# A gated delta-rule layer on one core: the second head's batches exchanged, products on all four quarters of the array, the decayed state made on GpSimd

## The reference, cut to what matters

```python
# x: 8 batches of 512 tokens, D = 256; 16 key heads, 32 value heads (2 per key head), head size 128, chunks of 64 tokens
qkvz = x @ W_qkvz                                   # per key head: q, k, two v, two z
q, k, v = silu(causal_conv1d(...)); g = cumulated log decay; beta = sigmoid(...)
attn = inverse of the unit lower triangle from k_beta k^T * decay_mask          # 64 by 64 for each chunk
for c in range(8):                                  # chunks, one after the other
    v_prime = value_corrected[c] - k_cumdecay[c] @ state
    out = (q[c] @ state) * g_exp + (q[c] k[c]^T * decay_mask) @ v_prime
    state = state * g_exp_last + (k[c] * k_decay)^T @ v_prime
out = rmsnorm(out * silu(z)) @ W_out
```

## Time and profile before

| | us |
|---|---|
| median of 3 runs | 4962.62 (4961.7 to 4965.15) |
| the profiled execution, its time | 4955.99 |
| its span, first to last instruction | 4954.2 |
| PE busy | 4628.7 (93%) |
| DVE busy | 3573.7 (72%) |
| ACT busy | 3072.0 (62%) |
| POOL busy | 694.4 (14%) |
| mean granted TensorE clock | 0.986 |

### The profile page before, as it was taken

The page is one execution under the profiler, slowest core; times in us unless marked ns, Lnnn a source line. Parts: engine busy times, 40 slices in busy tenths (PEclk is TensorE's granted clock), DMA queues, the critical chain, the costliest instruction groups (busy, mean ns, idle before and its releaser), DMA issues.

```text
span 4954.2 us, 144941 instructions
## 1 busy us (share of the span) xinstructions
PE 4628.7 (93%) x54288; PEld 3167.2 (64%) x54320; DVE 3573.7 (72%) x7576; ACT 3072.0 (62%) x7979; POOL 694.4 (14%) x680
## 2 busy tenths in 40 slices
PE   4998999999999899999999899999999899999998
PEld 2555666666666566666666566666666666666666
DVE  7554677777777677777777677777777677777776
ACT  2333666666666566666666566666666566666665
POOL 0000111111111111111111111111111111111111
PEclk8999999999999999999999999999999999999999
DMA  2111222222223222222223222222223222222221
GB/s 61 41 35 63 63 69 55 60 66 61 68 56 77 66 69 53 61 66 61 69 50 79 69 61 56 65 66 62 56 60 82 68 59 58 64 67 61 69 59 34
DMA packets 760100, 305.22 MB, mean 62 GB/s; under 512 B 672880, under 2 KB 716016, under 8 KB 749168
## 3 DMA queue, kind: packets, MB, share of 16 engines
q1 hardware_dynamic: 620144, 287.40, 23.5%
q10 hardware_dynamic: 139264, 8.42, 1.8%
HBM read 216.96 MB, written 66.07 MB: 57 GB/s over the span
## 4 chain that ended last, share of the span: by engine, by line
issue 56%; PE 27%; POOL 8%; DVE 4%; ACT 2%; DMA 1%; SPq 1%; POOLq 0%; DVEq 0%; ACTq 0%
PE pj L660 5%; POOL rout L1559 4%; PE dsb L819 3%; PE pj L655 2%; POOL gb L1550 2%; POOL kn L1555 2%; PE pot L605 2%; PE dsb L791 1%; PE pot L777 1%; PE ms L693 1%; PE pod L803 1%; PE ms L589 1%; PE pot L748 1%; PE pj L589 1%; PE pod L760 1%
## 5 line engine op out<-in xcount | busy, mean ns | idle before, releaser
L660 PE MATMUL pj<-xnT,wt 128*128 128x512 f32 x2048 | 1022.2, 622 | 34.0 <-DMA cw<-in_L_attn_conv_weight 20.6
L1292 DVE SCALAR_TENSOR_TENSOR cy<-xpad,cw,cy 128x1024 f32<-128x1024 f32 x768 | 976.2, 1278 | 7.9 <-ACT cy L1003 0.9
L1559 POOL TENSOR_TENSOR rout<-rin,expo 128x2 f32<-128x2 f32 x512 | 358.3, 700 | 3737.4 <-DVE rin L1443 3737.4
L1429 DVE SCALAR_TENSOR_TENSOR st<-st,gel,dsb 128x128 f32<-128x128 f32 x1536 | 430.9, 343 | 288.0 <-PE dsb L791 285.1
L819 PE MATMUL dsb<-wo,yT 128*128 128x256 f32 x2048 | 575.0, 403 | 13.2 <-issue 12.1
L660 PEld LDWEIGHTS pj<-xnT,wt 128*128 128x128 f32 x2048 | 351.7, 191 | 363.8 <-issue 349.0
L1002 ACT ACTIVATE xpad<-pj 128x512 f32<-128x512 f32 x512 | 305.5, 597 | 359.1 <-PE pj L660 359.1
L655 PE MATMUL pj<-wt,xnT 128*128 128x256 f32 x2048 | 509.9, 392 | 0.0
L1062 ACT ACTIVATE yT<-dsb 128x256 f32<-128x256 f32 x512 | 203.2, 397 | 469.0 <-PE dsb L810 467.5
L819 PEld LDWEIGHTS dsb<-wo,yT 128*128 128x128 f32 x2048 | 348.0, 189 | 117.8 <-issue 89.6
L655 PEld LDWEIGHTS pj<-wt,xnT 128*128 128x128 f32 x2048 | 368.3, 189 | 84.6 <-issue 44.3
(11 more groups left out here) (174 smaller groups left out, 8009.7 us busy)
## 6 DMA issues: line engine op xcount, KB each, us to landing
qge<-ge_rows SPq DMA_DIRECT2D x64, 1024.0 KB, 7.1
wt<-in_L_attn_W_qkvz SPq DMA_DIRECT2D x64, 768.0 KB
gb<-g_rows SPq DMA_DIRECT2D x128, 256.0 KB
a_d<-at SPq DMA_DIRECT2D x64, 512.0 KB, 2.6
wo<-in_L_attn_W_out SPq DMA_DIRECT2D x64, 256.0 KB, 2.7
x_d<-xpair SPq DMA_DIRECT2D x128, 128.0 KB, 1.8
ap_<-a_d SPq DMA_DIRECT2D x512, 16.0 KB, 1.8
dd<-x_d SPq DMA_DIRECT2D x512, 16.0 KB, 2.1
```

Source lines behind the costliest of these rows:

```text
L660: last = mm(pj[n % 2][:, :], wt[:, k, col:col + DH], batch(xnT, k, i), start=(k == 0), stop=(k == KD - 1))
L1292: stt(y, x[:, :, tap:tap + SEQ], cw[:, kind, tap:tap + 1], y, ALU.mult, ALU.add).then_inc(S["conv"], 1)
L1429: last = stt(st[:, (c + 1) % 2, b, h, :], st[:, c % 2, b, h, :], gel[:, p, h, b * NC + c:b * NC + c + 1], dsb[:, b, h * DH:(h + 1) * DH], ...
L1559: tt(rout[:, :], rin[:, :], expo[:, 0, 0:GRP], ALU.pow).then_inc(S["routs"], 1)
```

## The change: what it does, and the diff

1. For the second value head (h = 1) the two batches change places in the residual, in W and in the gated output (`home`). `solve` and `intra` then use all four 64 by 64 tiles: h = 0 on the diagonal, h = 1 off it, into another PSUM bank. The banks are laid out anew (`quad`). `key_state` becomes four products of 128 columns for two of 256, with the batches of h = 1 picked in exchanged order.
2. `output_rows` turns h = 1 back: it is now a product with an identity whose halves are exchanged (`cst[:, h*CH:...]`), and for h = 0 with the plain identity, in place of two transposes.
3. z is projected as before; ACT writes it exchanged. A z eviction of 128 by 512 becomes one of 128 by 2x128 and two of 64 partitions. For the first z fill (chunks 0, 1) the second part stands behind the SiLU and the squares of k, and `pcopy` counts only after it. The v evictions become four of 128 by 128 for two of 128 by 256. The v1 convolution holds its batches in exchanged places.
4. `update_state` was four instructions (state times decay plus increment, 128 by 128 each). POOL now multiplies the state by its decay (`decay_state`, chunks 1 to 6), and DVE adds the increment in one instruction.
5. The first fixpoint round no longer waits for the DMAs of eturn (DVE's second `add_round` does) but for all three negated copies. `decayed_squares(1)` moves from piece 18 to 17, one convolution tap from 17 to 18, and the first two `add_round` from piece 20 to 21, behind the residual of chunk 7.
6. In `last_tile` and at chunk 0 some waits move; the setup's layouts of g and of the columns change with the new order of units.

```diff
-        dsb = ctx.enter_context(nc.psum_tensor("dsb", [P, NB, 512], F32))
-        pch, pds = dsb[:, 0, :], dsb[:, 1, :]
-        pot = bank("pot")
-        pod = bank("pod")
-        pkw, po = pot, pod
+        quad = ctx.enter_context(nc.psum_tensor("quad", [P, 4, 512], F32))
+        pot, pod, pch, pds = (quad[:, n, :] for n in range(4))
+        po = quad[:, 0:2, DH:2 * DH]
+        pod_rows = quad[:, 0, 2 * DH:2 * DH + D]
+        pw = quad[:, 1:3, 0:DH]
+        pks = quad[:, 2, 0:GRP * DH]
+        pyt = quad[:, 3, 0:GRP * DH]
+        pstate = quad[:, 2:4, GRP * DH:2 * GRP * DH]
...
-                    loaded(pe, d_et, g, GRP * NBLK)
-                    after(pe, "pneg", g, 2)
+                    after(pe, "pneg", g, 3)
                 else:
                     after(pe, "yadd", g, 2 * r)
-                    if r == 1:
-                        after(pe, "pneg", g, 3)
                 apart(pe)
                 src = yy if r else ee
                 for v in range(8):
                     cut = slice(v * CH, (v + 1) * CH)
                     for b in range(NB):
                         straight = tile_product(ms[0][half(b), cut], b, pbd[half(b), v, :], src[half(b), v, :], b)
-                        if r == 1:
-                            turned = tile_product(ms[1][half(1 - b), cut], 1 - b, pback[half(b), v, :],
-                                                  yy[half(b), 8 + v, :], b)
-                        else:
-                            rhs = yy[half(1 - b), 8 + v, :] if r else eturn[half(1 - b), v, :]
-                            turned = tile_product(ms[1][half(b), cut], b, pbd[half(1 - b), 8 + v, :], rhs, 1 - b)
+                        lhsT = pback[half(b), v, :] if r == 1 else pbd[half(b), 8 + v, :]
+                        turned = tile_product(ms[1][half(1 - b), cut], 1 - b, lhsT, src[half(b), 8 + v, :], b)
...
             def key_state(g, p, c):
                 after(pe, "ss_", g, c)
                 apart(pe)
-                for b in range(NB):
-                    last = mm(pkw[half(b), 0:GRP * DH], kq[:, p, c, b, :],
-                              st[:, c % 2, b, :, :].rearrange("p h d -> p (h d)"), start=True, stop=True,
-                              tile_position=(0, b * CH))
+                for h in range(GRP):
+                    for b in range(NB):
+                        last = mm(pks[half(b), h * DH:(h + 1) * DH], kq[:, p, c, home(b, h), :],
+                                  st[:, c % 2, home(b, h), h, :], start=True, stop=True, tile_position=(0, b * CH))
                 last.then_inc(S["ks"], 1)
...
-                for h in range(GRP):
-                    for b in range(NB):
-                        rhs = rr[half(b), h, :] if c else vb[p][half(b), h, :]
-                        last = mm(pkw[half(b), (GRP + h) * DH:(GRP + h + 1) * DH], bda[half(b), p, c * GRP + h, :],
-                                  rhs, start=True, stop=True, tile_position=(b * CH, b * CH))
+                for a in range(NB):
+                    for h in range(GRP):
+                        rhs = rr[half(a), h, :] if c else vb[p][half(a), h * NC, :]
+                        last = mm(pw[half(home(a, h)), h, :], bda[half(a), p, h * NC + c, :], rhs,
+                                  start=(c == 0 or h == 1), stop=True, skip_group_check=True,
+                                  tile_position=(a * CH, home(a, h) * CH))
...
             def intra(g, p, c):
-                if c == 0:
-                    before(pe, "og", g)
                 if c == NC - 1:
                     after(pe, "wev", g, NC)
+                    after(pe, "accs", g, c - 3 + 1)
                 apart(pe)
-                for h in range(GRP):
-                    for b in range(NB):
-                        last = mm(po[half(b), h * DH:(h + 1) * DH], it[half(b), p, c * GRP + h, :], ww[half(b), h, :],
-                                  start=(c == 0), stop=True, skip_group_check=True, tile_position=(b * CH, b * CH))
+                for b in range(NB):
+                    for h in range(GRP):
+                        last = mm(po[half(home(b, h)), h, :], it[half(b), p, h * NC + c, :], ww[half(b), h, :],
+                                  start=(c == 0), stop=True, skip_group_check=True,
+                                  tile_position=(b * CH, home(b, h) * CH))
                 last.then_inc(S["op"], 1)
...
             def output_rows(g, p, j):
                 after(pe, "ysc", g, j + 1)
                 for h in range(GRP):
-                    last = tp(dsb[:, 1, (GRP + h) * DH:(GRP + h + 1) * DH], zz[p][:, j, h, :], ident)
+                    last = mm(pyt[:, h * DH:(h + 1) * DH], zz[p][:, j, h, :], cst[:, h * CH:h * CH + P],
+                              start=True, stop=True)
                 last.then_inc(S["yt"], 1)
 
-            def out_project(g, p, j):
+            def out_project(g, p, j, bank_cleared):
                 if j == 0:
                     after(pe, "wos", g, 1)
                 after(pe, "yte", g, j + 1)
                 all_but_last(pe, "accs", g, j)
                 for h in range(GRP):
-                    last = mm(dsb[:, 0, GRP * DH:GRP * DH + D], yT[:, h, :], wo[:, p, h, :],
-                              start=(h == 0), stop=(h == GRP - 1))
+                    last = mm(pod_rows, yT[:, h, :], wo[:, p, h, :], start=(h == 0 and not bank_cleared),
+                              stop=(h == GRP - 1), skip_group_check=True)
...
-                    for v in range(2):
-                        c = 2 * i + v
-                        last = fn(vb[p][:, c * GRP:(c + 1) * GRP, :].rearrange("p h d -> p (h d)"),
-                                  src[:, v * GRP * DH:(v + 1) * GRP * DH], ACT.Copy, scale=kn[:, c:c + 1])
+                    for v in range(4):
+                        c, h = 2 * i + v // GRP, v % GRP
+                        last = fn(vb[p][:, h * NC + c, :], src[:, v * P:(v + 1) * P], ACT.Copy, scale=kn[:, h, c:c + 1])
                 elif kind == "z":
-                    last = fn(zz[p][:, 2 * i:2 * i + 2, :, :].rearrange("p c h d -> p (c h d)"), src[:, :], ACT.Silu)
+                    z = src[:, :].rearrange("p (c h d) -> p c h d", c=2, h=GRP)
+                    if part != 1:
+                        last = fn(zz[p][:, 2 * i:2 * i + 2, 0, :], z[:, :, 0, :], ACT.Silu)
+                    if part != 0:
+                        for b in range(NB):
+                            last = fn(zz[p][half(1 - b), 2 * i:2 * i + 2, 1, :], z[half(b), :, 1, :], ACT.Silu)
+                    if part == 0:
+                        return
                 else:
...
                         if n == 3:
                             silu(g, p, 0)
                             squares(g, p, 0)
-                        empty_ring(g, p, n)
+                            empty_ring(g, p, 2, 1)
+                        empty_ring(g, p, n, 0 if n == 2 else None)
...
+                if (r, n) == (0, 1):
+                    loaded(dve, d_et, g, GRP * NBLK)
+                add = eturn[:, :, :] if n and r != 1 else ee[:, us, :]
                 if r < 2:
...
             def update_state(g, p, c):
                 after(dve, "ds", g, c + 1)
-                src = dsb[:, :, 0:GRP * DH]
+                src = pstate
                 dst = st[:, (c + 1) % 2, :, :, :].rearrange("p b h d -> p b (h d)")
                 if c:
-                    if c == 1:
-                        loaded(dve, d_ge, g, 1)
-                    for b in range(NB):
-                        for h in range(GRP):
-                            last = stt(st[:, (c + 1) % 2, b, h, :], st[:, c % 2, b, h, :],
-                                       gel[:, p, h, b * NC + c:b * NC + c + 1], dsb[:, b, h * DH:(h + 1) * DH],
-                                       ALU.mult, ALU.add)
-                    last.then_inc(S["ss_"], 1)
+                    after(dve, "sdecs", g, c)
+                    tt(dst, src, sdec[:, :, :, :].rearrange("p b h d -> p b (h d)"), ALU.add).then_inc(S["ss_"], 1)
                 else:
                     dve.tensor_copy(dst, src).then_inc(S["ss_"], 1)
...
                     join_left(g)
-                for n, at_s in enumerate((2, 3, 3, 8, 8, 9, 15, 15, 17, 17, 18, 20)):
+                if s == 17:
+                    decayed_squares(g, p, 1)
+                for n, at_s in enumerate((2, 3, 3, 8, 8, 9, 15, 15, 17, 18, 18, 20)):
                     if s == at_s:
                         convolve(g, n // 3, n % 3 + 1)
-                for n, at_s in enumerate((20, 20, 22, 22, 23, 23)):
+                for n, at_s in enumerate((22, 22, 23, 23)):
                     if s == at_s:
-                        add_round(g, p, n // 2, n % 2)
+                        add_round(g, p, 1 + n // 2, n % 2)
 
             def front_urgent(g, hk, s):
                 if s == 15:
                     join_right(g)
                     turn_inverse(g)
-                if s == 18:
-                    decayed_squares(g, hk % 2, 1)
```

(13 more changed lines are left out.)

## The result

The changed kernel takes **5255.62 us** (median of 4 runs, 5228.63 to 5275.48); the kernel before, measured beside it, 4962.16 (4958.58 to 4965.15). The ratio is 1.0589, with a 95% interval of 1.0543 to 1.0636. The forecast of 5085 had the sign right. The time lies above the whole stated range, which ended at 5170.

The account below looks back on a forecast made before the run. PE, busy 93% of the span, was taken to bound the kernel. To the profiled 4956 us came +72 (63 heads), -3 (last head), +54 (clock) and 6.6 (median of the runs): 5085 us, range 4985 to 5170.

Parts of the forecast that it names:

- Products on four tiles: PE's solve and intra get shorter, output_rows longer: -0.24 us a chunk, -1.9 us a head.
- Rival (d): The four tiles don't overlap, so solve and intra stay as they are: 5327 us, chance 0.03.
- The first z fill: Chunk 1: PE idles 2.9 us before the second q fill, waiting for ACT's late second half: +2.65 us a head.
- The v evictions: ACT needs eight instructions for four in the first two v fills, delaying PE's bank: +0.6 us (0 to 0.8).
- Waits that go: PE's waits for decayed_squares and for eturn's DMAs both go: -1.0 us a head (-0.5 to -1.4).
- Chunk 7: W's copy on ACT stands behind a SiLU and the longer output_rows, so solve's gain is partly lost: +0.1 us.
- The state update: POOL's decay_state holds up DVE's convolutions, delaying the residual in chunks 1 and 3: +0.7 us a head (0 to 1.6).
- The sum without the clock: All terms of a head together: +1.15 us, in 63 heads +72 us.
- The clock: PE's new idle time halves the clock for 3.4 us in every second head, losing 1.7 us each: +54 us.
- Rival (b): The clock falls in nearly every head, or POOL holds up more of DVE: 5139 us, chance 0.12.
- rival (c): ACT is through before PE reaches the second q fill, so that wait is gone: faster, 4865 us, chance 0.10.

Follow-up runs that it names:

- z_whole_dve: z_whole with the state's decay back on DVE (four instructions, nothing on POOL): 5046.84 us.
- keep_busy: The changed kernel with one unread projection product on PE just ahead of the second q fill: 5150.92 us.
- z_whole: The changed kernel with the second half of the first z eviction back in front of the SiLU and squares of k on ACT: 5046.93 us.
- z_gram_t: z_gram with output_rows for the first head of the pair as a transpose again: 4974.11 us.
- z_gram: z_whole_dve with PE's products of the keys with each other put ahead of the sums of their squares: 4981.51 us.
- before_gram: The kernel before with PE's products of keys (and of queries) with each other put ahead of the sums of their squares: 4937.94 us.
- z2_dve_t: z_whole_dve with the first z fill emptied a piece earlier and the first head's output_rows as a transpose again: 5100.7 us.

## Where the prediction was right and where it failed

**Products on four tiles: right, a little too high.** PE in later chunks of the changed kernel, where nothing waits:

```profile
2673.16 0.45 PE L804 MATMUL quad<-ww,arena 64*64 64x128 f32 x8
2673.54 1.98 PE L669 MATMUL pj<-xnT,wt 128*128 128x512 f32 x4
...
2677.44 0.61 PE L812 MATMUL quad<-cst,arena 128*128 128x128 f32 x4
2677.98 0.45 PE L778 MATMUL quad<-rr,bda 64*64 64x128 f32 x8
2678.36 1.99 PE L664 MATMUL pj<-wt,xnT 128*128 128x256 f32 x8
```

From the start of L778, and of L804, to the next row it is 0.38 us, for 0.59 before. That is -0.42 a chunk for -0.48. L812 takes 0.54 for 0.31, +0.23 for +0.24. Together -0.19, and the step from the fifth `solve` to the sixth shows just that, 7.94 to 7.76. Eight chunks of -0.18: -1.4, forecast -1.9. Rival (d) is out.

**The first z fill: right.** Idle 2.73 us for the 2.9 forecast, in each head, and L673's wait at the keys' squares gone. What was overlooked is small: the squares of the queries come later on ACT as well, and L682 waits 0.36 us for them in 63 heads, where it was 0.13 before: +0.23.

**The v evictions:** 0.35 for 0.6, too high, but within its bounds.

**Waits that go: failed.** The step said -1.0 a head, because both waits of the earlier trace rows go, "1.4 in such a head". They went. But the two rows add up to 48.1 us, 0.76 for each of 63 heads, so even for nothing in return the step claimed too much: it took the price of a head that has both waits for the mean. And all idle time in front of the block products (L693, now L702), added up over the trace, is 98 us before and 103 after. PE's wait for the landing of dd grew from 8.4 us to 25.9, that for the negation (L1056) from 0.7 to 14.4, that for `at` (L1429) from 1.5 to 5.2, and the gaps put down to issue by the rest. The forecast named the next two in line, and had no row for their price. That is the largest error outside the clock: 63 us.

**Chunk 7** cost 0.13 for 0.1 (L804 waits 18.8 us for W, 10.4 before).

**The state update: right in the mechanism, too high in the effect.** 0.67 us more for a convolution was forecast as 0.7 (0.95 less 0.34 is 0.61 by its own numbers). PE pays 0.34 of it and not 0.7, by the two steps in z_whole_dve, and 0.18 more since the state is now waited for: 14.6 us for the copy of the first one, L1451, for 1.5 before, and 17.6 for 6.1 with the later ones. Why this copy is late is not shown. DVE and POOL in the head shown above:

```profile
2786.99 0.68 DVE L1451 COPY st<-quad 128x512 f32<-128x512 f32 x1
...
2787.91 1.96 DVE L1309 SCALAR_TENSOR_TENSOR cy<-xpad,cw,cy 128x1024 f32<-128x1024 f32 x1
```

```profile
2787.74 1.05 POOL L1583 TENSOR_TENSOR sdec<-st,gel 128x512 f32<-128x512 f32 x1 [2.90 <-DVE st L1451]
```

The Trainium skill's rule (SBUF — State Buffer, Who interferes with whom), that one of the two engines blocks the other for the length of its instruction, fits: the convolution starts 0.17 us behind L1583, of which 0.88 are then left, and takes 0.67 more than without it (that it stands still for just that time is argued, not shown). What the rule can't say is what the engine held up had in hand.

**The sum without the clock:** -1.4 + 2.55 + 0.23 + 0.35 + 0.1 + 0.13 + 0.52 = +2.5, and 2.33 by the count, 2.6 by keep_busy. The forecast had +1.15.

**The clock: failed.** The step read "3.4 us at half speed lose 1.7. I take every second head". Both factors were low. It was three heads in four, 46 of 63, and the stretches last 3.4, 6.8 or 10.2 us, 6.4 on average behind L669: 292 us in 46 stretches. Counted, that is 2.46 us a head for 0.86; keep_busy gives 2.2 by its steps, and 1.7 by its whole time, which holds what it lost elsewhere. The length of 3.4 came from the one stretch in the earlier trace rows, and there PE's idle time was 2.0 us. The error of 171 us is thus some 85 to 100 for the clock and 74 to 90 for the rest, the waits that go above all.

Rival (b), the clock in nearly every head at 5139, came nearest, and the range ended 86 us too early since it had no case in which the wait brings longer stretches than the one seen, nor one in which the waits that go give nothing. That the sign came out right rests on the z fill alone, the one term of this size; without it the forecast would have been a gain (rival (c), 4865), and z_whole shows a loss of 84 us.

**Open:** why 17 of the 63 equal idle times leave the clock alone; whether the transpose in z_gram_t gains anything; what slows the end of the head in keep_busy and z_whole; which part of the change costs the 44 us left in z_gram, beyond the 0.62 us a head at L669.

## What to carry to other kernels

An idle time on PE costs more than its length: a wait of 2.7 us in each head cost 2.55 us and again some 2.1 in clock, so the first question to a change is whether it makes PE stand, and not how many instructions it saves. A wait that goes is worth at most its total over all heads, and nothing is won until the next in line at the same instruction has a price of its own. And before an instruction is moved forward in an engine's order, follow what it is moved past through the other engines; moving independent work into the gap on the waiting engine (before_gram) was the only edit that came out faster than the kernel before.

## What the runs showed of the hardware

- Around the end of an idle time of 2.73 us the granted clock fell to 0.50 in 46 of 63 cases, for 3.4 to 10.2 us, through up to 9.6 us of uninterrupted work. A product that nobody reads, put into that time, took the time at half clock from 358 us to 96 and the program from 5256 to 5151.
- A product in place of a transpose of 128 by 128 costs about 0.1 us more, start to start: two of them 0.54 us for 0.31.
- Eight matmul records of 128 columns on four tiles take 0.38 us up to the start of the next row, on two tiles 0.59, although two of the four tiles write into one bank.
- ACT's table load, 1.28 us, stands in front of the z eviction in each head, before and after, and was in no sum; in z2_dve_t it stands ahead of the output squares, and DVE, held up behind them, made PE wait.
- A convolution on DVE (two inputs in SBUF) took 1.96 us beside POOL's product of 128 by 512, and 1.28 in all 768 cases with that product gone.
